# A feed-forward block with two sets of PSUM banks, the residual added on TensorE and the last normalisation on ScalarE

## What is computed

```python
unperm = jnp.argsort(perm)
t = x.reshape(b * l, Dm)[:, perm].reshape(b * l, h, d)   # 512 tokens, 16 heads, 32
t = jnp.einsum('bhd,hdm->bhm', t, up)                    # m = 128
t = jax.nn.gelu(t, approximate=False)
t = jnp.einsum('bhm,hmd->bhd', t, down)
out = t.reshape(b * l, h * d)[:, unperm].reshape(b, l, Dm)
...
x = _layernorm(x + out, axis=-1)
```

## Time and profile before

| what | us |
|---|---|
| median of 3 runs | 900.6 (899.0 to 900.81) |
| the profiled execution, its own time | 902.15 |
| its span (first to last record) | 900.3 |
| TensorE busy in the span | 838.8 (93%) |
| ScalarE busy | 460.8 (51%) |
| VectorE busy | 564.4 (63%) |
| GpSimd busy | 512.3 (57%) |
| mean granted TensorE clock | 0.976 of full speed |
| the feed-forward stage, in the span | 858.6 to 900.3 |

### The profile page before, as it was taken

The page is one execution under the profiler, slowest core; times in us unless marked ns, Lnnn a source line. Parts: engine busy times, 40 slices in busy tenths (PEclk is TensorE's granted clock), DMA queues, the critical chain, the costliest instruction groups (busy, mean ns, idle before and its releaser), DMA issues. The chain is left out here.

```text
span 900.3 us, 15076 instructions
## 1 busy us (share of the span) xinstructions
PE 838.8 (93%) x4833; PEld 701.5 (78%) x4833; DVE 564.4 (63%) x1505; ACT 460.8 (51%) x977; POOL 512.3 (57%) x655
## 2 busy tenths in 40 slices
PE   7978998889989679999999999999999999999975
PEld 5756766667768568888888888888888888888753
DVE  5455665656543367767766766766766766767535
ACT  5464655346513265545546545555555555555343
POOL 5475745355521297576576576576576566545711
PEclk9999999999999799999999999999999999999979
DMA  6413223112203542112112112112112101000011
GB/s 220 131 60 106 60 70 119 36 59 71 71 1 94 168 143 83 36 49 81 37 47 82 35 47 78 38 47 69 47 47 66 51 1 61 17 1 1 1 24 47
DMA packets 48462, 56.22 MB, mean 62 GB/s; under 512 B 4622, under 2 KB 29724, under 8 KB 48412
## 3 DMA queue, kind: packets, MB, share of 16 engines
q1 hardware_dynamic: 48412, 55.59, 19.8%
HBM read 41.95 MB, written 13.63 MB: 62 GB/s over the span
## 5 line engine op out<-in xcount | busy, mean ns | idle before, releaser
L1080 POOL TENSOR_SCALAR prob<-prob,x_rinv 128x768 f32<-128x768 f32 x128 | 116.2, 908 | 166.3 <-DVE x_rinv L1255 166.3
L1197 ACT ACTIVATE pT_hi<-bank 128x512 fp32r<-128x512 f32 x192 | 114.5, 597 | 95.5 <-PE bank L1412 95.0
L1176 ACT ACTIVATE prob<-bank,x_nm,q_rms 128x768 f32<-128x768 f32 x128 | 127.1, 993 | 49.3 <-DVE x_nm L1249 48.9
L1246 DVE TENSOR_REDUCE x_mx<-bank 128x1 f32<-128x768 f32 x128 | 122.1, 954 | 25.1 <-PE bank L1370 24.9
L1308 DVE TENSOR_TENSOR pT_lo<-bank,pT_hi 128x512 fp32r<-128x512 f32 x192 | 130.3, 679 | 8.6 <-ACT pT_hi L1197 7.1
L1412 PE MATMUL bank<-ident,prob 128*128 128x128 f32 x768 | 115.7, 273 | 6.0 <-POOL prob L1080 6.0
L1412 PEld LDWEIGHTS bank<-ident,prob 128*128 128x128 f32 x768 | 95.3, 141 | 18.3 <-POOL prob L1080 7.1
L398 ACT ACTIVATE s_self<-s_self,nm_self 128x128 f32<-128x128 f32 (+1 forms) x128 | 57.0, 447 | 71.7 <-DVE nm_self L511 71.7
L48 PE MATMUL bank<-pT_hi,xv_hi 128*128 128x512 f32 x192 | 86.7, 452 | 0.9 <-DVE pT_lo L1308 0.8
L50 PE MATMUL bank<-pT_hi,xv_lo 128*128 128x512 f32 x192 | 75.8, 395 | 0.0
L49 PE MATMUL bank<-pT_lo,xv_hi 128*128 128x512 f32 x192 | 75.5, 393 | 0.0
(11 more groups left out here) (195 smaller groups left out, 2082.8 us busy)
## 6 DMA issues: line engine op xcount, KB each, us to landing
wo_raw<-in_Wo SPq DMA_DIRECT2D x8, 1024.0 KB, 5.3
wq_raw<-in_Wq SPq DMA_DIRECT2D x7, 1024.0 KB, 5.5
v_by_head<-v_st SPq DMA_DIRECT2D x12, 512.0 KB, 3.2
kT_by_head<-kT_st SPq DMA_DIRECT2D x12, 512.0 KB, 3.4
xk_raw<-kT_by_head SPq DMA_DIRECT2D x16, 384.0 KB, 3.2
xv_raw<-v_by_head SPq DMA_DIRECT2D x16, 384.0 KB, 3.2
wq_raw<-in_w_attn SPq DMA_DIRECT2D x12, 256.0 KB, 3.5
xk_raw<-in_ctx SPq DMA_DIRECT2D x8, 256.0 KB, 3.8
```

Source lines behind the costliest of these rows:

```text
L1080: nc.gpsimd.tensor_scalar(prob[:, s, :], prob[:, s, :], rinv[:, s:s + 1], 1.0, ALU.mult, ALU.mult)\
L1176: nc.scalar.activation(prob[:, s, :].rearrange("p (a e) -> p a e", a=2), bank[:, at:at + 2, 0:HALF], ACT.Exp, bias=nm[:, s:s + 1], scale=q ...
L1197: nc.scalar.activation(pT_hi[:, a, :], bank[:, turn.bank[s, what, a], :], ACT.Copy)\
L1246: nc.vector.reduce_max(mx[:, s:s + 1], bank[:, at:at + 2, 0:HALF], AX.XY)\
```

## The change

Only `feed_forward` changes.

- ScalarE starts the stage with a Gelu of one column (`gelu_warm`), so the table load stands there.
- Hidden products of odd groups go to banks 4 to 7, of even groups to 0 to 3; `hid` has room for all four groups. The order on TensorE is up 0, 1, 2, down 0, up 3, down 1, down 2, then the rest. The results of the down products go to the banks 4, 0, 1, 4 (`Y_BANK`), the outputs of the scatter to the banks 2, 3, 5, 6 (`Z_BANK`).
- Where a down product lies in a bank of the next hidden set, up 3 waits until VectorE has split it (y_lo).
- yT_hi of groups 0 to 2 is made by VectorE (a cast) and not by ScalarE; the last one stays on ScalarE.
- The scatter goes group by group over two or four token tiles ("quads") in place of tile by tile.
- The residual comes in by TensorE: x is split into res_hi (ScalarE, 4 copies) and res_lo (GpSimd, 4 operations), and two identity matmuls per token tile, 8 in all, open the sum of each output bank. VectorE's four additions are gone.
- VectorE takes its statistics from PSUM. It makes shift = -mean * rstd, one column per tile, and ScalarE normalises from PSUM into x (Identity with bias and scale) in place of VectorE.

```diff
-        hid = t.sb("hid", [P, 2, HPT, TOK])
+        hid = t.sb("hid", [P, KT, HPT, TOK])
...
+        Y_BANK = (4, 0, 1, 4)
+        Z_BANK = (2, 3, 5, 6)
...
@@ gpsimd
+            for j in range(TT):
+                pool.wait_ge(res_his, j + 1)
+                nc.gpsimd.tensor_tensor(res_lo[:, j, :], x[:, j, :], f32(res_hi[:, j, :]), ALU.subtract).then_inc(res_los, 1)
...
@@ scalar
+            nc.scalar.activation(warm[:], ident[:, 0:1], ACT.Gelu).then_inc(warm_done, 1)
...
             def gelus(i):
                 for r in range(HPT):
-                    if r == 0 and i >= 2:
-                        act.wait_ge(y_ps, i - 1)
                     act.wait_ge(h_ps, HPT * i + r + 1)
-                    nc.scalar.activation(hid[:, i % 2, r, :], bank[:, r, :], ACT.Gelu).then_inc(h_out, 1)
+                    nc.scalar.activation(hid[:, i, r, :], bank[:, 4 * (i % 2) + r, :], ACT.Gelu).then_inc(h_out, 1)
+            nc.scalar.activation(ident_r[:], ident[:], ACT.Copy).then_inc(ident_out, 1)
+            for j in range(TT):
...
+                nc.scalar.activation(res_hi[:, j, :], x[:, j, :], ACT.Copy).then_inc(res_his, 1)
...
+            act.wait_ge(y_ps, KT)
+            nc.scalar.activation(yT_hi[:, KT - 1, :], bank[:, Y_BANK[KT - 1], :], ACT.Copy).then_inc(last_y_hi, 1)
+            for i in range(TT):
+                act.wait_ge(shift_made, i + 1)
+                nc.scalar.activation(x[:, i, :], bank[:, Z_BANK[i], :], ACT.Identity, bias=shift[:, i:i + 1],
+                                     scale=k.rstd[:, TT + i:TT + i + 1]).then_inc(ln_made, 1)
...
@@ vector
             def statistics(i):
-                nc.vector.bn_stats(k.stats[:, i, :], x[:, i, :]).then_inc(y_stats, 1)
+                dve.wait_ge(z_ps, i + 1)
+                nc.vector.bn_stats(k.stats[:, i, :], bank[:, Z_BANK[i], :]).then_inc(y_stats, 1)
...
+            def make_shift(i):
                 dve.wait_ge(rstd_made, i + 1)
-                nc.vector.tensor_scalar(x[:, i, :], x[:, i, :], k.mv[:, 1, i, 0:1], k.rstd[:, TT + i:TT + i + 1],
-                                        ALU.subtract, ALU.mult).then_inc(ln_made, 1)
+                nc.vector.tensor_scalar(shift[:, i:i + 1], k.mv[:, 1, i, 0:1], k.rstd[:, TT + i:TT + i + 1], -1.0,
+                                        ALU.mult, ALU.mult).then_inc(shift_made, 1)
...
+            def result_split(i):
+                if i < KT - 1:
+                    dve.wait_ge(y_ps, i + 1)
+                    nc.vector.tensor_copy(yT_hi[:, i, :], bank[:, Y_BANK[i], :]).then_inc(y_hi, 1)
+                    dve.wait_ge(y_hi, i + 1)
+                else:
+                    dve.wait_ge(last_y_hi, 1)
...
@@ tensor
             def up_products(i):
-                pe.wait_ge(t_lo, i + 1)
                 if i == 0:
+                    pe.wait_ge(t_lo, 1)
                     pe.wait_ge(up_los, 1)
+                elif i == 1:
+                    pe.wait_ge(t_lo, KT)
                 else:
-                    pe.wait_ge(h_out, HPT * i)
+                    pe.wait_ge(h_out, HPT * (i - 1))
+                if i == 3:
+                    pe.wait_ge(y_lo, 1)
...
             def down_products(i):
-                pe.wait_ge(h_out, HPT * (i + 1))
+                pe.wait_ge(h_out, min(HPT * KT, HPT * (i + 1) + (1 if i < 2 else 0)))
...
+            def scatter_group(i, js):
+                pe.wait_ge(y_lo, i + 1)
+                for j in js:
+                    w = slice(j * P, (j + 1) * P)
+                    nc.tensor.matmul(bank[:, Z_BANK[j], :], yT_hi[:, i, w], scatter[:, i, :], start=False, stop=False)
+                    last = nc.tensor.matmul(bank[:, Z_BANK[j], :], yT_lo[:, i, w], scatter[:, i, :], start=False,
+                                            stop=i == KT - 1)
...
+            def residual(js):
+                pe.wait_ge(ident_out, 1)
+                pe.wait_ge(res_los, TT)
+                for j in js:
+                    nc.tensor.matmul(bank[:, Z_BANK[j], :], ident_r[:], res_hi[:, j, :], start=True, stop=False)
+                    nc.tensor.matmul(bank[:, Z_BANK[j], :], ident_r[:], res_lo[:, j, :], start=False, stop=False)
...
+            up_products(0)
+            up_products(1)
+            up_products(2)
+            down_products(0)
+            up_products(3)
+            down_products(1)
+            down_products(2)
+            residual((0, 1))
+            scatter_group(0, (0, 1))
+            scatter_group(1, (0, 1))
+            down_products(3)
+            residual((2, 3))
+            scatter_group(0, (2, 3))
+            scatter_group(1, (2, 3))
+            scatter_group(2, range(TT))
+            scatter_group(3, range(TT))
```

More of the change, by code:

```diff
@@ L1460, in feed_forward @@
         tT_lo = t.sb("tT_lo", [P, KT, TOK], F32R)
-        hid = t.sb("hid", [P, 2, HPT, TOK])
+        hid = t.sb("hid", [P, KT, HPT, TOK])
+        warm = t.sb("gelu_warm", [P, 1])
+        ident_r = t.sb("ident_r", [P, P], F32R)
+        res_hi = t.sb("res_hi", [P, TT, D], F32R)
+        res_lo = t.sb("res_lo", [P, TT, D], F32R)
+        shift = t.sb("ln_shift", [P, TT])
         yT_hi = t.sb("yT_hi", [P, KT, TOK], F32R)
@@ L1512, in permuted_hi @@
                 nc.scalar.activation(tT_hi[:, i, :], bank[:, 4 + i, :], ACT.Copy).then_inc(t_hi, 1)
-            def result_hi(i):
-                act.wait_ge(y_ps, i + 1)
-                nc.scalar.activation(yT_hi[:, i, :], bank[:, 4 + i, :], ACT.Copy).then_inc(y_hi, 1)
             def gelus(i):
                 for r in range(HPT):
-                    if r == 0 and i >= 2:
-                        act.wait_ge(y_ps, i - 1)
                     act.wait_ge(h_ps, HPT * i + r + 1)
-                    nc.scalar.activation(hid[:, i % 2, r, :], bank[:, r, :], ACT.Gelu).then_inc(h_out, 1)
+                    nc.scalar.activation(hid[:, i, r, :], bank[:, 4 * (i % 2) + r, :], ACT.Gelu).then_inc(h_out, 1)
+            nc.scalar.activation(ident_r[:], ident[:], ACT.Copy).then_inc(ident_out, 1)
+            for j in range(TT):
+                if j >= 2:
+                    act.wait_ge(x2_made, j - 1)
+                nc.scalar.activation(res_hi[:, j, :], x[:, j, :], ACT.Copy).then_inc(res_his, 1)
             for i in range(KT):
@@ L1558, in permuted_lo @@
                 nc.vector.tensor_tensor(tT_lo[:, i, :], bank[:, 4 + i, :], f32(tT_hi[:, i, :]), ALU.subtract).then_inc(t_lo, 1)
-            def result_lo(i):
-                dve.wait_ge(y_hi, i + 1)
-                nc.vector.tensor_tensor(yT_lo[:, i, :], bank[:, 4 + i, :], f32(yT_hi[:, i, :]), ALU.subtract).then_inc(y_lo, 1)
+            def result_split(i):
[5 more added lines that the diff above has]
+                    dve.wait_ge(last_y_hi, 1)
+                nc.vector.tensor_tensor(yT_lo[:, i, :], bank[:, Y_BANK[i], :], f32(yT_hi[:, i, :]), ALU.subtract)\
+                    .then_inc(y_lo, 1)
             for i in range(KT):
@@ L1566, in _ @@
             for i in range(KT):
-                result_lo(i)
+                result_split(i)
             for i in range(TT):
-                dve.wait_ge(z_ps, i + 1)
-                nc.vector.tensor_tensor(x[:, i, :], bank[:, i, :], x[:, i, :], ALU.add).then_inc(y_sum, 1)
-                dve.wait_ge(y_sum, i + 1)
                 statistics(i)
                 if i > 0:
-                    normalise(i - 1)
-            normalise(TT - 1)
+                    make_shift(i - 1)
+            make_shift(TT - 1)
         @block.tensor
@@ L1606, in up_products @@
                         q = slice(FD * r, FD * (r + 1))
-                        done = nc.tensor.matmul(bank[:, r, :], weights[q, i, :], rows[q, i, :], start=first, stop=last)
+                        done = nc.tensor.matmul(bank[:, 4 * (i % 2) + r, :], weights[q, i, :], rows[q, i, :], start=first,
+                                                stop=last)
                         if last:
@@ L1614, in down_products @@
                     pe.wait_ge(down_in, 16)
-                pe.wait_ge(h_out, HPT * (i + 1))
+                pe.wait_ge(h_out, min(HPT * KT, HPT * (i + 1) + (1 if i < 2 else 0)))
                 for r in range(HPT):
-                    last = nc.tensor.matmul(bank[FD * r:FD * (r + 1), 4 + i, :], down[:, i, r, :], hid[:, i % 2, r, :],
+                    last = nc.tensor.matmul(bank[FD * r:FD * (r + 1), Y_BANK[i], :], down[:, i, r, :], hid[:, i, r, :],
                                             start=True, stop=True)
                 last.then_inc(y_ps, 1)
+            def scatter_group(i, js):
[5 more added lines that the diff above has]
+                                            stop=i == KT - 1)
+                    if i == KT - 1:
+                        last.then_inc(z_ps, 1)
+            def residual(js):
[4 more added lines that the diff above has]
+                    nc.tensor.matmul(bank[:, Z_BANK[j], :], ident_r[:], res_lo[:, j, :], start=False, stop=False)
             for b in range(B):
```

8 lines of the change are left out of this document (3 added, 5 removed).

## The result

The changed kernel takes 899.09 us (median of 14 runs, 894.15 to 900.97), the kernel before 901.68 (14 runs, 899.0 to 903.95). The ratio of the runs is 0.9963 with a 95% interval of 0.9946 to 0.9979, so in this measurement it is faster by 0.2 to 0.5% (the two medians alone, 2.59 us apart, give 0.9971). Predicted were 898.3, counted from the first three runs' 900.6, and a gain of 2.3 us. The first interval holds 2.3 us (0.9974) and the second ends at it; the second also holds 1, no change at all. So whole times bound the gain only loosely, and its size is read from the stage in the traces. What is known of the runs' scatter is told at the end.

What follows compares the result with a forecast made beforehand. TensorE is busy 93% of the span, but the feed-forward stage was taken as bound by alternating Gelus and products. The parts moved its last result from 897.93 to 895.60, so 900.6 - 2.3 = 898.3 us, range 896.8 to 900.8.

Steps and rivals of the forecast that it cites:

- part 1: Stage start: the table load moved there makes TensorE's gather products start 0.20 us later, bounds 0 and 0.34.
- rival C: Stage start: the load holds ScalarE longer than its 1.28 us, adding 1.3, total 899.6; chance 0.06.
- part 2: Up products and Gelus on two bank sets: first Gelu at 871.91 against 872.67, fourth up group at 877.59.
- The new wait for y_lo: Before the fourth up group: TensorE waits until VectorE splits down product 0 in bank 4, a pause of 1.5 us.
- part 3: TensorE without a pause from 877.59 through up, down, residual and scatter, ending about 890.98 against 893.98: 3.0 us won.
- part 4: Tail on VectorE, GpSimd and ScalarE: 5.98 us, ending at 895.60 before 897.93, 2.3 won; VectorE's tail late next.
- rival B: TensorE's clock falls in the two-bank section, up to 902.5 us; chance 0.08 for slower, 0.04 for a short fall.
- D: Tail takes back more: statistics at a period of 1.4 us, +0.9, and a store pushed 0.4, total 899.6; chance 0.16.
- E: Wait before up 3 on bank 4 grows by 2.3 us beyond 1.5, gain gone, total 900.6; chance 0.08.

Runs made afterwards that it cites:

- e8: The changed kernel again without an edit; ratio to the kernel before 0.9989 (0.9974 to 1.0005), last normalise ends 24.98 us after the first up product.
- e1: The changed kernel without the one-column Gelu, so the table load stands in front of the first Gelu; ends 25.99 us after the first up product, 1.02 later.
- e6: The changed kernel with the fourth hidden group in banks 5, 6, 7, 0 and down results in 4, 1, 4, 7; ends 23.84 us after the first up product.
- e7: The changed kernel with the banks of e6 and token tiles 0 and 1 finished early; ratio to the kernel before 0.9940 (0.9917 to 0.9963).
- e2: The changed kernel with the old tail: VectorE adds the residual and normalises, no identity passes; ends 26.44 us after the first up product, 1.47 later.
- e5: The changed kernel with its last 16 scatter matmuls by token tile in place of by group; ends 23.56 us after the first up product, 1.41 earlier.
- e9: e2 with the scatter in an order that finishes tiles 0 and 1 early; ends 24.56 us after the first up product.
- e3: The kernel before with only the one-column Gelu added at the stage's start; ends 26.05 us after the first up product, 1.22 less.

## Why the prediction was right

**The load (part 1).** The sum had +0.20 at the first gather product for the load in its new place. In the profiled execution it is 0.00: 862.62 - 859.27 = 3.35 against 3.36 before. The load and the one-column Gelu took what was forecast (1.28 and 0.20), but the first x2T copy started 0.10 before that Gelu's end, and ScalarE and VectorE did the first two copies and differences as pairs (1.21 and 1.32 us), which caught up the rest. There is luck in the 0.00. It holds where the stage begins at 1.2 GHz, as in the profiles that the prediction and this sum rest on, since the transposes then feed the copies slowly (3.65 for the 16). In e8 the clock was 1.00 from the start, the transposes took 1.94, and TensorE waited 1.39 for the split that stands behind the load:

```profile
857.59 1.94 PE L1602 MATMUL bank<-ident,x_rows 128*128 128x128 f32 x16 [3.17 <-PEq L898]
...
860.91 0.38 PE L1609 MATMUL bank<-x2T_hi,wq_hi 128*128 128x256 f32 x1 [1.39 <-DVE x2T_lo L1569]
```

e1, without the load at the start, has no such wait, and its first gather product comes at 2.67 behind the first transpose:

```profile
856.55 2.97 PE L1601 MATMUL bank<-ident,x_rows 128*128 128x128 f32 x16 [3.19 <-PEq L898]
...
859.22 0.58 PE L1608 MATMUL bank<-x2T_hi,wq_hi 128*128 128x256 f32 x1
```

e6 and e7, with the load and nearly the same transposes (3.01 and 2.92), come to 3.33 and 3.32, with waits of 0.32 and 0.40. So there the load costs 0.65 in its new place, outside of the prediction's bounds of 0 to 0.34, and the counting from the first up product doesn't show it. The gain on the other side is shown by e1, 1.02; by an estimate from these rows, some 0.4 of it is left in such an execution. For the 1.39 of e8 there is no execution without the load that started as fast, so what it cost stays open.

The Trainium skill ("ScalarE: Activation LUTs", What ACT_TABLE_LOAD costs) counts a drain of about 1.38 us on top. No run here shows it: in the kernel before the load starts 0.02 behind the last copy's end (870.76 + 0.60 to 871.38) and the Gelu 0.01 behind the load's. So rival C fell.

**Two bank sets (part 2).** The first Gelu was worked out at 1.05 behind the first up product and came at 1.00; the fourth up group at 6.73 (877.59 - 870.86), and it came at 6.71. That is closer than its parts: the third up group began at 3.11 where the sum had 3.26, and TensorE took up the split 0.15 behind its end (877.33 + 0.69 to 878.17) where the sum had 0.05. The new wait for y_lo was named with its place, and e6 priced it: 1.13. The cast from PSUM, for which no row stood, took 0.69.

**TensorE's run (part 3).** Its end was forecast 20.12 behind the first up product and came at 20.27. Of the parts, the three down groups took 2.85 in place of 3.00, down 1 and 2 being 1.85 together, and each of the three changes between down products and residual or scatter took about 0.1 more than the interval of 0.233 (880.93 to 881.26, 883.60 to 883.92, 884.92 to 885.25).

**The tail (part 4).** Forecast 5.98 from the first bn_stats to the end, measured 6.07 (890.36 to 896.43). bn_stats with a PSUM operand took 0.69, the two-operand normalise 0.78, GpSimd 0.55 each time, as forecast for a tail without VectorE's wide tensor_scalar from SBUF: in e2, which has it again, GpSimd took 0.78 for three of the four. The sentence that VectorE's tail is late next is what e5 and e9 confirm.

**The clock (rival B).** The pauses of 0.51, 0.65 and 1.63 left it at 1.00. The Trainium skill ("TensorE: Matmul & The Clock Gate", A second HAM failure mode: psum-queue depth-cycling) tells of another kernel whose clock fell and rose by frequent short pauses between groups of matmuls. This kernel had three such pauses and no fall, so the trace does not show it here. e3 shows that the rival was not far: a fall came behind a pause of 2.25, while the prediction had rows for 1.18 and 1.28 without a fall and for 3.24 with one.

**Rivals D and E** fell with the same rows: bn_stats every 1.13 and not 1.4, and the wait 1.63 and not 3.8. From the last normalise to the end of the span it took 2.47 in place of 2.37, but that is no cost of the closer stores: it is 2.37 to 2.47 in the five executions with the old tail and 2.40 to 2.48 in the seven with the new one.

**The sum.** The forecast of 2.3 was for the whole stage: 2.53 behind the first up product (27.27 to 895.60 - 870.86 = 24.74), less 0.20 ahead of it. The runs gave 2.30 behind it, less 0.13 ahead of it (12.19 for 12.06, all of it in the gather products, of which 11 and not 10 began at 1.2 GHz), so 2.17 of 2.33. The mechanism came as forecast; behind the first up product the sum was 0.23 too good, 0.14 of it up to the first bn_stats (18.90 for 18.76) and 0.09 in the tail. That the 2.30 looks like the 2.3 is a coincidence of two different counts.

## What to carry to other kernels

An earlier end on the busy engine pays only as far as the engine behind it has been given its work early: finish output tiles one after the other, as far apart as the pace of the tail, and do not let all of them come at the end. In this case the order of 16 matmuls was worth 1.4 us. The old tail in a good order (24.56) was as good as the new tail in a poor one (24.97), and the new tail in a good order was ahead of them by 1.5 and 1.9 us (23.10). When a result is put in a bank of the next set, look at what the next user then waits for: a bank plan whose next bank comes free one Gelu into the group, and not behind two steps of VectorE, took off 1.1 us here. Work of a stage that depends on nothing, like a table load, belongs in a gap where its engine's next work is not late, and whether it is late can differ between executions: with a faster start the load here came onto the chain in its new place. ScalarE idles for 10.89 us ahead of it, in the block before; a load there was not tried.

## What the runs showed that was not expected

The runs of one kernel lie up to 7 us apart, three times the change. The trace shows where: in front of the middle. For four profiled executions these are the first qT_hi copy of the cross-attention (at 354 to 361 us) and the first transpose of the feed-forward stage, of the kernel before, the changed one, e5 and e7:

```profile
358.18 0.59 ACT L1169 ACTIVATE qT_hi<-bank 128x512 fp32r<-128x512 f32 x1
...
858.60 3.65 PE L1583 MATMUL bank<-ident,x_rows 128*128 128x128 f32 x16 [3.17 <-PEq L898]
```

```profile
358.85 0.59 ACT L1169 ACTIVATE qT_hi<-bank 128x512 fp32r<-128x512 f32 x1
```

```profile
354.05 0.59 ACT L1169 ACTIVATE qT_hi<-bank 128x512 fp32r<-128x512 f32 x1
...
854.45 3.65 PE L1602 MATMUL bank<-ident,x_rows 128*128 128x128 f32 x16 [3.19 <-PEq L898]
```

```profile
360.88 0.59 ACT L1169 ACTIVATE qT_hi<-bank 128x512 fp32r<-128x512 f32 x1
...
861.32 2.92 PE L1603 MATMUL bank<-ident,x_rows 128*128 128x128 f32 x16 [3.19 <-PEq L898]
```

The 500 us between them are alike to 0.04 (500.42, 500.42, 500.40, 500.44), while the first 358 us, whose code none of these kernels changes, differ by 6.8. The granted clock goes with it: in 80 to 200 us its mean was 0.97 in the kernel before and 1.00 in e5, the execution that was earliest. In the 14 runs of the changed kernel the four of mean clock 0.977 took 899.2 to 900.7 where the two fastest (894.15 and 894.58) had 0.984 and 0.985. Over all twelve profiled executions, the five with 0.97 in that window began the stage at 858.60 to 861.32, and the seven with 0.99 or 1.00 at 854.45 to 857.59. That the clock's falls in the first block are the cause fits these rows but was not tried by itself, and it stays open what else differs there.

The second thing is in e3: the clock fell behind a pause of 2.25 us, but only 0.7 us after TensorE had taken up work again, so that most of the slow matmuls were not those right behind the pause but the down products and the up group after them.
